# High one-hots of a degree histogram laid out with the columns of a round innermost

## The reference

```python
def block0(x, edge_index, edge_attr, ...):
    agg = segment_sum(edge_attr, dst, n)            # sums of the edges' rows by target node
    h = relu(concat([x, agg]) @ W1 + b1); h = relu(h @ W2 + b2); h = h @ W3 + b3
    return layernorm(h) * ln_w + ln_b

def block1(x, ...):                                 # two layers of attention over the graph
    for l in range(2):
        xn = layernorm(x) * g + b
        deg = segment_sum(ones(E + n), concat([src, arange(n)]), n)     # the degree histogram
        deg = (deg - deg.mean()) / (std(deg, ddof=1) + 1e-6)
        pos = xn @ Wpos + bpos + deg[:, None] * Wdeg + bdeg
        q, k, v = projections of xn + pos, 8 heads of 16
        att = clip(sum(q[dst] * k[src]) / 4, -50, 50); alpha = softmax of att over the edges of a dst
        x = x + segment_sum(v[src] * alpha, dst) @ Wo + bo
        x = x + gelu(layernorm(x) @ W1 + b1) @ W2 + b2
    return x
```

## Time and profile before

| | us |
|---|---|
| median of 3 runs | 3471.74 |
| lowest and highest run | 3464.63, 3478.25 |
| span of the profiled execution (its only time given) | 3472.7 |
| stage of the edge sums, in the profile | about 27 to 330 |

### The profile page before, as it was taken

The page is one execution under the profiler, slowest core; times in us unless marked ns, Lnnn a source line. Parts: engine busy times, 40 slices in busy tenths (PEclk is TensorE's granted clock), DMA queues, the critical chain, the costliest instruction groups (busy, mean ns, idle before and its releaser), DMA issues.

```text
span 3472.7 us, 60241 instructions
## 1 busy us (share of the span) xinstructions
PE 2377.0 (68%) x13853; PEld 2027.0 (58%) x13854; DVE 1981.1 (57%) x7060; ACT 1704.5 (49%) x4472; POOL 1820.8 (52%) x1968
## 2 busy tenths in 40 slices
PE   6998774567667676777667746666666666666667
PEld 6988333556556565656556635556565565565556
DVE  7887782455555555555556625555555455554555
ACT  6765653345445444545445434354444445454444
POOL 5642655655555555555555245556555555555552
PEclk9999885778878878878888867788778778787788
DMA  7865232222322222222223122222222222222221
GB/s 211 242 207 172 88 106 85 85 77 84 89 86 84 84 79 85 79 86 82 82 83 88 45 72 83 82 81 84 81 77 78 81 79 81 77 81 81 78 84 37
DMA packets 180176, 323.48 MB, mean 93 GB/s; under 512 B 38740, under 2 KB 93991, under 8 KB 179892
## 3 DMA queue, kind: packets, MB, share of 16 engines
q0 software_dynamic: 80208, 216.22, 21.7%
q1 hardware_dynamic: 98948, 103.44, 9.7%
q10 hardware_dynamic: 736, 0.93, 0.1%
HBM read 288.09 MB, written 20.71 MB: 89 GB/s over the span
## 4 chain that ended last, share of the span: by engine, by line
another core or an unknown queue 15%; PE 13%; issue 10%; DVE 8%; DVEq 3%; ACT 3%; ACTq 0%; DMA 0%; SPq 0%
PE bank L2080 5%; DVE aggregate L2120 3%; PE bank L2071 2%; PE bank L1729 2%; PE bank L1723 1%; DVE arena L2128 1%; ACT arena L2013 1%; PE bank L2056 1%; PE bank L1720 1%; DVE arena L2148 1%; DVEq L2109 1%; DVE arena L2162 1%; DVEq L2120 1%; PE bank L1718 1%
## 5 line engine op out<-in xcount | busy, mean ns | idle before, releaser
L1992 POOL DMA_INDIRECT arena<-kv_rows,idx_stage x1612 | 1540.8, 956 | 1344.6 <-DVE arena L2128 798.4
L2080 PE MATMUL bank<-arena 128*128 128x136 f32 x3328 | 698.7, 359 | 654.1 <-DVE aggregate L2120 551.8
L2120 DVE TENSOR_TENSOR aggregate<-bank,aggregate 128x136 f32 x1664 | 493.9, 297 | 1017.6 <-remote 851.3
L2080 PEld LDWEIGHTS bank<-arena 128*128 128x128 f32 x3328 | 589.1, 249 | 746.1 <-DVE aggregate L2120 419.9
L2071 PE MATMUL bank<-queries,arena 128*128 x3328 | 547.5, 317 | 82.0 <-DVE arena L2148 53.6
L2071 PEld LDWEIGHTS bank<-queries,arena 128*128 128x128 f32 x3328 | 509.9, 233 | 91.3 <-issue 90.8
L2013 ACT ACTIVATE arena<-iota_n,at_negdst 128x128 f32<-128x128 f32 x1664 | 527.7, 395 | 3.8 <-DMA kv_rows<-arena 2.0
L1777 ACT ACTIVATE arena<-bank 128x256 f32<-128x256 f32 (+1 forms) x225 | 85.0, 379 | 731.8 <-remote 454.8
L2056 PE MATMUL bank<-ident,arena 128*128 128x128 f32 x1664 | 325.7, 329 | 106.1 <-issue 63.0
L2148 DVE TENSOR_TENSOR arena<-bank,arena 128x512 f32<-128x512 f32 x416 | 284.6, 684 | 152.8 <-remote 68.2
L2037 ACT ACTIVATE arena<-arena 128x32 f32<-128x32 f32 x416 | 92.8, 223 | 556.0 <-DVE arena L2177 336.3
(11 more groups left out here) (322 smaller groups left out, 2796.3 us busy)
## 6 DMA issues: line engine op xcount, KB each, us to landing
arena<-in_edge_attr_dram SPq DMA_DIRECT2D x244, 256.0 KB
arena<-kv_rows,idx_stage POOLq DMA_INDIRECT x1612
kv_rows<-arena SPq DMA_DIRECT2D x12, 512.0 KB, 3.8
kv_rows<-arena SPq DMA_DIRECT2D x24, 256.0 KB, 2.2
arena<-in_x_dram SPq DMA_DIRECT2D x12, 256.0 KB, 4.0
x_rows<-arena SPq DMA_DIRECT2D x12, 256.0 KB, 2.9
x_stream<-arena SPq DMA_DIRECT2D x12, 256.0 KB, 2.3
queries<-arena SPq DMA_DIRECT2D x12, 256.0 KB, 2.7
```

Of the source, the lines that this page charges most:

```text
L1992: pool.indirect_dma_start(kv[:, n, :], None, kv_dram[l], bass.IndirectOffsetOnAxis(idx_stage[:, half % 2, n:n + 1], 0)).then_inc(Z.kv_in[s ...
L2080: pe.matmul(sums_of(j), sel[:, r % SEL_SLOTS, j, :], msg[:, r % 2, j, :], start=True, stop=True).then_inc(Z.sum, 1)
L2120: dve.tensor_tensor(a, sums_of(j), a, ALU.add).then_inc(Z.added, 1)
```

## The change

The high one-hots get the low ones' layout, with the 13 columns innermost. VectorE compares the part of `hist_iota` for 49 tiles with the 13 codes, repeated for each tile, so that no operand has a step of zero in its innermost dimension. TensorE reads its moving operand at a step of 13 elements.

```diff
-        oh_hi = [o.rearrange("p (c n) -> p c n", c=HIST_ROUND) for o in oh_hi]
+        oh_hi = [o.rearrange("p (n c) -> p n c", c=HIST_ROUND) for o in oh_hi]
...
-                        last = pe.matmul(bank[:, 0, 0:NT], oh_lo[h][:, :, c], oh_hi[h][:, c, :], start=first and h == 0 and c == 0,
+                        last = pe.matmul(bank[:, 0, 0:NT], oh_lo[h][:, :, c], oh_hi[h][:, :, c], start=first and h == 0 and c == 0,
...
-                return dve.tensor_tensor(oh_hi[h], tile_iota[0:HIST_ROWS, 0:NT].unsqueeze(1).to_broadcast([HIST_ROWS, HIST_ROUND, NT]),
-                                         codes_of(src_hi, m).unsqueeze(2).to_broadcast([HIST_ROWS, HIST_ROUND, NT]), ALU.is_equal)
+                return dve.tensor_tensor(oh_hi[h], hist_iota[0:HIST_ROWS, 0:NT, :],
+                                         codes_of(src_hi, m).unsqueeze(1).to_broadcast([HIST_ROWS, NT, HIST_ROUND]), ALU.is_equal)
```

## The result

The changed kernel took 3492.39 us in the median of 5 runs (3490.18 to 3497.05), the one before 3471.74 (3464.63 to 3480.74, 5 runs on the same chip). The ratio is 1.0053, with a 95% interval of 1.0035 to 1.0071: 12 to 25 us slower. The forecast was 3467, with 3455 to 3489 as its range; the measured time is 3 us beyond the slower end, and the sign of the forecast was wrong.

What follows compares the result with a forecast made beforehand. The prediction took TensorE to bound the edge-sum stage, with short waits for VectorE. VectorE's terms of 5.1 us, taken as 5, and nothing for TensorE's strided read gave 3471.7 - 5 = 3467 us, range 3455 to 3489.

Steps and rivals of the forecast that it cites:

- what bounds the stage: Edge-sum stage: TensorE bounds it, busy 283 of 294 us, with no hole in a steady round of 4.42 us.
- VectorE's instruction: High one-hots on VectorE (L1068): 818 ns falls to 513, saving 305 ns in each of 62 instructions.
- 0.3 + 2.1 + 2.7: VectorE's gain reaching the path: start 0.3, seven short waits 2.1, six waits for an addition 2.7; sum 5.1 us.
- (c): TensorE's six waits for an addition, 6.5 us: earlier rounds' shorter high one-hots save 0.45 us each, 2.7 us.
- (b): TensorE's seven short waits, where slot 1 waits for a selection: nearly all of 0.35 us each goes, 2.1 us.
- some 3: Part of a TensorE slowdown, in us, swallowed by the rounds in which TensorE waits for VectorE.
- the moving read's price: Histogram matmuls (L1040): reading the moving operand at a step of 26 bytes costs nothing, hidden by the stationary load.
- second rival: Moving read has its own price, 21 ns becoming 84: 24 ns more a matmul, 3488 us; chance 0.05.
- Overlap of load and moving read: Histogram matmuls: stationary load and moving read run beside each other, so 21 of 60 ns is covered.
- first rival: Both strided reads share a way: 21 to 23 ns more a matmul, 14 us more, 3486 us; chance 0.13.
- The sign that was to tell the two rivals apart: L1040 matmuls 80 ns or more apart: load's shortest duration unchanged at 136 means own price; longer means sharing.

Runs made afterwards that it cites:

- e2: Kernel before, with only TensorE's moving read of the high one-hots changed to a step of 13 elements: 3493.22 us, ratio 1.0056.
- e1: Changed kernel, but TensorE reads 49 contiguous elements of the high one-hots, leaving only VectorE's half: 3467.85 us against 3473.37 of before, ratio 0.9972.
- e4: Kernel before, with a round's 13 matmuls reading the stationary operand at steps of 1 to 13 elements, moving contiguous: 3484.57 us against 3473.37, executed once.
- e11: Kernel before, each histogram matmul split into two of 64 stationary columns, still at a step of 13 elements: 3523.36 us against 3478.45, executed once.
- e3: A round's 13 matmuls read the moving operand at steps of 1 to 13 elements, stationary contiguous: 3490.88 us against 3473.37 of before, executed once.
- e9: High one-hots in three groups of five columns, moving read at a step of 10 bytes, low ones as before: ratio 0.9995 to before.
- e13: Both one-hots in pairs of columns (4-byte step), each round's codes at a pitch of 14 instead of 13: 3517.39 us against 3524.96 of before, ratio 0.9982.
- e5: High one-hots in seven groups of two columns, moving read at a step of 4 bytes, low ones as before: ratio 0.9986 to before.

## Why the prediction was wrong, point by point

**Right: what bounds the stage.** TensorE is full, each ns a matmul costs its 0.8 us. 34 ns in each of 12 distances is 0.41 us a round, the period rose by 0.40, and over 61 periods that is 24.6 us; e2's stage lost 19.0, so 5.6 us of it were swallowed where TensorE had waited (forecast: some 3): all its waits in the rounds were 14.4 us before and are 8.4 in e2.

**Right: VectorE's instruction**, 510 ns against 513. **Too large: its worth.** I gave it 5 us, as 0.3 + 2.1 + 2.7. e1 shows 2.2; the changed kernel against e2 shows 2.0, or 3.7 without the 1.7 us that the clock took. The terms that were too large are (c), the six waits for an addition, of which e1 still has 6.1 us where I had taken 2.7 away, and (b), the short ones, which fell from 2.5 to 1.6 and not by 2.1. I read (c) so that the gains of the earlier rounds don't carry over, because VectorE is back in step with TensorE before its work between bodies begins; no run was made for it.

**The failed step: the moving read's price, taken as nothing.** Its basis was the sentence that in the stationary load "a column at the step costs 56 / 128 = 0.44 ns, what a moving column costs now", "which speaks for no penalty at all". e4 and e11 show what that number was, if the two halves of e11 are read as side by side: four columns fetched in 1.8 to 1.9 ns, not one in 0.44. The rows of before had the clue. 128 contiguous columns of bf16 loaded in 15 ns, 0.12 each, a quarter of a moving column's 0.45; so a load of bf16 has a width that the moving read has not, and the two can't be compared column by column. What can be compared is the factor: 56 / 15 = 3.7. Times 21 ns it is 78, beyond the cover of 60. I had that as the second rival (84 ns, 24 more a matmul, 3488 us, within 5 of the result) and gave it 0.05, with the reason that the 15 was "the special case". It was, but that was the reason for the factor and not against it. That its 3488 lies so near the result is partly luck: the time is that of before with the price added, without the 5 us that I gave VectorE's half, and with them it would have been 3483; the price itself, 24 ns, was 10 too low.

**Overlap of load and moving read** was right for this change: e3's 90 ns with a cheap load and the 94 with a strided one differ by 4. The first rival falls as a cause. The sign that was to tell the two rivals apart came as written for the second: more than 80 ns apart, the load's shortest duration unchanged at 136.

**The range** ended at 3489, as the second rival was sized at 24 ns a matmul. Measured are 34: the read's own 90, and 4 more, which the two strided reads side by side may cost (e3 against the changed kernel; the 4 ns were not traced further).

**The total** of 20.6 us is above the stage's 17.0. The two profiles differ by 15.4, and the interval begins at 12. I take the rest for spread of the later stages, which no experiment changed; that is not shown.

## What to carry to other kernels

A layout that makes VectorE's operand run contiguously can take TensorE's operand apart: look at the distance between two columns that a matmul reads. Count a moving operand by the lines of 16 bytes that it touches, at 1.84 ns each here, and compare with what else fills the distance between matmuls. With 49 columns a step of 4 bytes was free, 6 bytes cost 35 ns, 8 bytes 47 to 49, and 16 bytes or more 90. A load of 60 ns covers up to 10 bytes (e9), one of 26 covers only 4 (e13). And price a step by the ratio of strided to contiguous on the same path, as the load and the moving read fetch at different widths.

## What else the runs showed

The one-hot instruction on VectorE (`is_equal` of two bf16 sources, one of them a short run of codes, repeated) costs, by these runs, about 150 ns and then 1.04 ns for every word of 4 bytes that a run of the codes touches. The 1.04 is (862 - 505) / 343, one word more in each of 343 runs of 2. Runs of 13 touch 7 words however they begin: 128 x 7 x 1.04 = 932, with 150 it is 1082 (1093 measured). Runs of 5 touch 3: 147 runs make 609 (611). Runs of 2 touch one word when they begin at a multiple of 4 bytes and two when not: 343 runs make 507 and 863 (505 and 862 measured). Runs of 4 touch 2 or 3: 196 runs make 558 and 762 (554 and 759). So an odd run length hides an odd start, and an even one doesn't.

The same program takes 3473 us on one chip, 3526 on another and 2698 on a third (medians of before, 21 to 27 runs each), while the stage of the edge sums with TensorE at the same spacing is 291 to 293 us on each (e1, e9, e5). The difference lies in what follows, which the study did not touch. The mean granted clock of an execution differs too, 0.92 to 0.95 in the runs of before at 2698 us and 0.80 to 0.81 in those at 3473 and 3526. Two chips with the same clock differ by 53 us all the same, and whether the clock is cause or consequence stays open.
